# A perceiver layer with eight experts: residual rows sorted in the experts' order, weighted and scattered by each expert pass, and three weight parts used whole

## The reference

```python
x = x + xattn(layernorm(x), ctx, ctx, ...)       # 4 x 128 rows of 512, context 4 x 2048 x 256
x = x + dss(layernorm(x), ...)                   # long convolution
# expert layer, 512 tokens, 8 experts, 512 -> 2048 -> 512, everything in float32
xn = layernorm(x)
probs = softmax(xn @ w_gate + b_gate); route_p = max(probs); route_idx = argmax(probs)
h = relu(xn @ W1[e] + b1[e]); y = h @ W2[e] + b2[e]
out = x + y[route_idx] * route_p
```

## Time and profile before

| | us |
|---|---|
| median of 3 runs | 450.99 |
| lowest, highest | 450.6, 452.78 |
| the profiled execution, its own time | 450.92 |
| its span, first to last instruction | 449.1 |
| passes, first product to last | 188.4 to 431.6 |
| after the last product | 17.5 |

### The profile page before, as it was taken

How to read it: one execution, slowest core, us unless ns; L and a number is a source line. 1 busy time by engine, 2 the same in 40 slices (tenths; PEclk the granted TensorE clock), 3 DMA queues, 4 the chain that set the end, 5 groups by cost and what they waited for, 6 DMA issues and landing times.

```text
span 449.1 us, 5478 instructions
## 1 busy us (share of the span) xinstructions
PE 398.2 (89%) x1620; PEld 272.0 (61%) x1620; DVE 319.3 (71%) x506; ACT 249.9 (56%) x379; POOL 36.2 (8%) x41
## 2 busy tenths in 40 slices
PE   0999999999998975699998999999999999999940
PEld 0855567587863454576765667667576766757620
DVE  2778758795425867577877978799697879969702
ACT  4789778581000020575775757667685776757500
POOL 2100000000000010000201002010020201002022
PEclk9999999999999985989999999999999999999985
DMA  7995280874459400100169997698997979500006
GB/s 249 418 420 221 88 348 1 329 277 161 170 191 398 159 7 0 50 0 0 38 237 367 371 397 259 241 362 326 355 368 283 351 299 352 194 0 23 1 23 187
DMA packets 33695, 95.71 MB, mean 213 GB/s; under 512 B 2691, under 2 KB 3331, under 8 KB 32133
## 3 DMA queue, kind: packets, MB, share of 16 engines
q1 hardware_dynamic: 30900, 91.61, 54.8%
q0 software_dynamic: 1136, 3.67, 2.4%
q10 hardware_dynamic: 1632, 0.11, 0.3%
HBM read 91.72 MB, written 3.67 MB: 212 GB/s over the span
## 4 chain that ended last, share of the span: by engine, by line
PE 82%; DVE 6%; ACT 4%; DMA 3%; issue 3%; POOL 1%; DVEq 1%; SPq 0%; POOLq 0%; ACTq 0%
PE bank L1443 46%; PE bank L1281 6%; PE bank L1262 5%; PE bank L1458 4%; PE bank L1291 3%; PE bank L1215 2%; DMA ring<-in_wq_t 2%; PE bank L1327 2%; PE bank L1303 2%; PE bank L1270 2%; DVE work L1106 1%; DVE w_lo L1125 1%; ACT ring L518 1%; PE bank L1334 1%; PE bank L1424 1%
## 5 line engine op out<-in xcount | busy, mean ns | idle before, releaser
L1125 DVE TENSOR_TENSOR w_lo<-ring,w_hi 128x1024 fp32r<-128x1024 f32 x108 | 135.0, 1294 | 9.2 <-ACT w_hi L683 9.2
L683 ACT ACTIVATE w_hi<-ring 128x1024 fp32r<-128x1024 f32 x108 | 112.8, 1055 | 35.8 <-PE bank L1443 35.3
L1443 PE MATMUL bank<-ring,work 128*128 128x512 f32 x144 | 67.8, 603 | 0.0
L1443 PE MATMUL bank<-w_hi,x_hi 128*128 128x512 f32 x144 | 49.3, 424 | 5.1 <-DVE w_lo L1125 5.1
L1443 PE MATMUL bank<-w_hi,x_lo 128*128 128x512 f32 x144 | 45.2, 396 | 0.0
L1443 PE MATMUL bank<-w_lo,x_hi 128*128 128x512 f32 x144 | 45.1, 395 | 0.0
L1443 PEld LDWEIGHTS bank<-ring,work 128*128 128x128 f32 x144 | 25.8, 189 | 25.6 <-issue 23.3
L708 ACT ACTIVATE h_hi<-work 128x512 fp32r<-128x512 f32 x36 | 22.7, 631 | 26.5 <-DVE work L1112 25.9
L1193 POOL TENSOR_TENSOR small<-small,work 128x512 f32<-128x512 f32 x9 | 17.2, 1914 | 241.2 <-ACT small L689 241.2
L1443 PEld LDWEIGHTS bank<-w_hi,x_hi 128*128 128x128 f32 x144 | 26.7, 192 | 14.5 <-DVE w_lo L1125 8.0
L1106 DVE COPY work<-bank 128x512 f32<-128x512 f32 x18 | 12.4, 688 | 27.1 <-PE bank L1443 27.1
(11 more groups left out here) (184 smaller groups left out, 555.5 us busy)
## 6 DMA issues: line engine op xcount, KB each, us to landing
ring<-in_w SPq DMA_DIRECT2D x32, 2048.0 KB, 9.6
ring<-in_ctx_turned SPq DMA_DIRECT2D x4, 2048.0 KB, 12.2
ring<-in_ctx SPq DMA_DIRECT2D x4, 2048.0 KB, 14.2
y_rows<-small POOLq DMA_DIRECT2D x9, 256.0 KB, 5.3
work<-in_b SPq DMA_DIRECT2D x8, 256.0 KB, 5.6
ring<-in_wq_t SPq DMA_DIRECT2D x1, 1024.0 KB, 8.9
x_sb<-in_x SPq DMA_DIRECT2D x1, 1024.0 KB, 11.3
out<-x_sb SPq DMA_DIRECT2D x4, 256.0 KB, 3.0
```

What stands on the lines that cost most here:

```text
L683: act.activation(w_hi[:, n % NSPLIT, :, :], weight_part(e, n), ACT.Identity).then_inc(hi_ready, 1)
L1125: dve.tensor_tensor(w_lo[:, n % NSPLIT, :, :], weight_part(e, n), w_hi[:, n % NSPLIT, :, :], ALU.subtract).then_inc(lo_ready, 1)
L1443: ins = pe.matmul(dst, kept, moved, start=start and g == 0 and q == 0, stop=stop and g == 1 and q == len(terms) - 1)
```

## The change

1. **Rows.** `x_sb` becomes `x_ext`, 514 columns a row: the residual, the gate's probability and the token's number. After the router POOL scatters its four blocks to the DRAM tensor `sorted_rows` in the experts' order and waits for them. `y_rows`, the gathers, the four weighted additions and SP's four writes are gone.
2. **A pass.** After the pass before has been scattered, POOL loads this window's 128 rows of `sorted_rows` into `x_rows_w` (which is block 0 of `x_ext`). DVE adds probability times the expert's bias to them as the last step of a pass (`bias_added`). In the next pass ACT's copy of the result multiplies by the probability, POOL adds the row block, and scatters the sum by an indirect DMA to the result at the tokens' numbers. The padding rows have a number beyond the result and are skipped.
3. **Parts.** `WHOLE` is (6, 14, 15). Parts 12 and 13 are halved now, 14 is whole; `h_hi` and `h_lo` of block 3 are no longer made, and o3 waits for the relu.
4. **Waits.** The wait on the earlier output block stands in `block_may_copy` only where that block has a whole part; so the copy of h3 no longer waits for o1. The waits on `h_lo` of odd blocks count one a pass.

```diff
-WHOLE = (6, 12, 13, 15)
+WHOLE = (6, 14, 15)
...
-    y_rows = nc.dram_tensor("y_rows", ((NB + 1) * P, D), F32, kind="Internal").ap()
+    sorted_rows = nc.dram_tensor("sorted_rows", ((NB + 1) * P, D + 2), F32, kind="Internal").ap()
...
-        x_sb = sb("x_sb", [P, NB, D])
+        x_ext = sb("x_ext", [P, NB, D + 2])
+        x_sb = x_ext[:, :, 0:D]
+        x_rows_w = x_ext[:, 0, :]
...
         def block_may_copy(eng, p, w, k):
             wait_block(eng, w, "h", 2 * k + p)
-            eng.wait_ge(h_lo_ready[p], 2 * w + k + 1)
-            wait_block(eng, w, "o", 2 * k + p - 2)
+            if p == 0 or k == 1:
+                eng.wait_ge(h_lo_ready[p], 2 * w + k + 1 if p == 0 else w + 2)
+            before = 2 * k + p - 2
+            if not {2 * BLOCKS.index(("o", before % 4)) + g for g in range(2)}.isdisjoint(WHOLE):
+                wait_block(eng, w, "o", before)
...
# ScalarE: outputs_copy(w), and the end of its pass
                 act.wait_ge(rows_sent, 16 * w + 16)
-                act.activation(y_out, bank[:, Y_BANK, :], ACT.Identity).then_inc(y_copied, 1)
+                act.wait_ge(sorted_sent, 16 * NB)
+                act.wait_ge(x_rows_ready, w + 1)
+                act.activation(y_out, bank[:, Y_BANK, :], ACT.Identity, scale=x_rows_w[:, D:D + 1]).then_inc(y_copied, 1)
...
                         block_copy(w, 1)
+                        for n in range(12, 14):
+                            split_high(e, w, n)
                         block_relu(e, w, 1)
                         block_high(w, 2)
-                        for n in (14,):
-                            split_high(e, w, n)
-                        block_high(w, 3)
...
# VectorE
+            def bias_added(e, w):
+                dve.wait_ge(x_rows_loaded, 16 * w + 16)
+                dve.wait_ge(b2_loaded[e % NB2], 16 * (e // NB2 + 1))
+                dve.scalar_tensor_tensor(out=x_rows_w[:, 0:D], in0=b2_sb[e % NB2], scalar=x_rows_w[:, D:D + 1],
+                                         in1=x_rows_w[:, 0:D], op0=ALU.mult, op1=ALU.add).then_inc(x_rows_ready, 1)
...
                         block_copy(w, 1)
+                        for n in range(12, 14):
+                            low_part(e, w, n)
                         block_low(w, 2)
                         block_relu(e, w, 1)
-                        low_part(e, w, 14)
-                        block_low(w, 3)
+                        bias_added(e, w)
...
# GpSimd, after its 17 value_loads
+            pool.wait_ge(rows_ready, 2)
+            pool.wait_ge(prob_ready, 1)
+            for b in range(NB):
+                pool.indirect_dma_start(sorted_rows, bass.IndirectOffsetOnAxis(ap=row_i[:, b:b + 1], axis=0),
+                                        x_ext[:, b, :], None).then_inc(sorted_sent, 16)
+            pool.wait_ge(sorted_sent, 16 * NB)
...
                         first_row = window_row(offsets[e], w - bounds[e])
+                        pool.wait_ge(y_copied, w + 1)
+                        pool.wait_ge(rows_sent, 16 * w + 32)
+                        pool.dma_start(x_rows_w, sorted_rows[bass.ds(first_row, P), :]).then_inc(x_rows_loaded, 16)
+                        pool.wait_ge(x_rows_ready, w + 2)
                         pool.wait_ge(y_copied, w + 2)
-                        pool.tensor_tensor(y_out, y_out, b2_sb[e % NB2], ALU.add).then_inc(y_added, 1)
+                        pool.tensor_tensor(y_out, y_out, x_rows_w[:, 0:D], ALU.add).then_inc(y_added, 1)
                         pool.wait_ge(y_added, w + 2)
-                        pool.dma_start(y_rows[bass.ds(first_row, P), :], y_out).then_inc(rows_sent, 16)
+                        pool.tensor_tensor(rstd, m_half, m_half, ALU.mult)
+                        pool.indirect_dma_start(out, bass.IndirectOffsetOnAxis(ap=x_rows_w[:, D + 1:D + 2].bitcast(U32), axis=0),
+                                                y_out, None, bounds_check=NB * LQ - 1, oob_is_err=False) \
+                            .then_inc(rows_sent, 16)
             pool.wait_ge(rows_sent, 16 * bounds[NE] + 32)
...
# TensorE: output(e, w, i)
-                pe.wait_ge(h_lo_ready[p], 2 * w + k + 2)
+                if i == 3:
+                    pe.wait_ge(h_relu[p], 2 * w + k + 2)
+                else:
+                    pe.wait_ge(h_lo_ready[p], 2 * w + k + 2 if p == 0 else w + 2)
```

More of the change, by code:

```diff
@@ L58 @@
 for _name, _n in (("ident", P), ("ones", P), ("cos_f", P), ("sin_f", P), ("cos_t", P), ("sin_t", P),
-                  ("pick", P + BL - 1), ("own", HG), ("earlier", P), ("iota", P), ("blocks", NB), ("rank_e", NE),
+                  ("pick", P + BL - 1), ("own", HG), ("token", NB), ("earlier", P), ("iota", P), ("blocks", NB), ("rank_e", NE),
                   ("before_e", (NE + 1) * NE)):
@@ L63 @@
 TABLE_COLS = _at
-COLS = 172
+COLS = 148
 K1 = 16
@@ L200, in perceiver_layer @@
         by_group = small[:].rearrange("p (g n) -> p g n", n=2 * HG)
-        zeros = work[:, 0:D]
+        pad_rows = work[:, 0:D + 2]
         k_time = small[:, 0:D]
@@ L233, in perceiver_layer @@
         step_l, phase_c = times_c[:, 0:AH + BL], times_c[:, AH + BL:]
-        step_mag, step_ph = col(AH + BL), col(AH + BL)
+        step_mag, step_ph = col(AH + BL), step_l
         bn6, mv = col(6), col(2 * NB)
@@ L257, in perceiver_layer @@
         fmax = route(100, 4)
-        psum_e, prob = route(104, 4), route(108, 4)
+        psum_e = route(104, 4)
+        prob = x_ext[:, :, D:D + 1].rearrange("p b o -> p (b o)")
+        token = x_ext[:, :, D + 1:D + 2].rearrange("p b o -> p (b o)").bitcast(U32)
         rt1 = TABLES["sin_f"][0]
@@ L320, in perceiver_layer @@
         y_copied, y_added, rows_sent = sem("y_copied"), sem("y_added"), sem("rows_sent")
-        gathered = [sem(f"gathered{b}") for b in range(NB)]
-        result_ready, result_sent = sem("result_ready"), sem("result_sent")
+        sorted_sent, prob_ready = sem("sorted_sent"), sem("prob_ready")
+        x_rows_loaded, x_rows_ready = sem("x_rows_loaded"), sem("x_rows_ready")
         def weight_place(j):
@@ L481, in _ @@
                 next_b2(e)
[L482 to L485, removed]
         @block.scalar
@@ L706, in block_high @@
                 act.wait_ge(h_relu[p], 2 * w + k + 2)
-                wait_block(act, w, "o", i - 2)
+                wait_block(act, w, "o", i - 2 if p == 0 else i - 4)
                 act.activation(h_hi[:, p, :, :], hid[p].rearrange("p (m s) -> p m s", m=HB_CH), ACT.Identity) \
@@ L1080, in _ @@
             dve.tensor_copy(row_i, slot).then_inc(rows_ready, 1)
-            one_ahead = [*h_copied, *t_filled, *h_relu, *h_lo_ready, y_added]
+            dve.tensor_copy(token, table("token")).then_inc(rows_ready, 1)
+            one_ahead = [*h_copied, *t_filled, *h_relu, *h_lo_ready, y_added, x_rows_ready]
             for i, s in enumerate(one_ahead + PARTS * [parts_used]):
@@ L1118, in block_low @@
                 p, k = i % 2, i // 2
-                dve.wait_ge(h_hi_ready[p], 2 * w + k + 1)
+                dve.wait_ge(h_hi_ready[p], 2 * w + k + 1 if p == 0 else w + 1)
                 dve.tensor_tensor(h_lo[:, p, :, :], hid[p].rearrange("p (m s) -> p m s", m=HB_CH), h_hi[:, p, :, :],
@@ L1169, in inverse_root @@
                     .then_inc(rstd_ready, 1)
-            pool.memset(zeros, 0.0).then_inc(zeros_ready, 1)
-            pool.wait_ge(zeros_ready, 1)
+            pool.memset(pad_rows[:, 0:D + 1], 0.0).then_inc(zeros_ready, 1)
+            pool.memset(pad_rows[:, D + 1:D + 2], 1.0).then_inc(zeros_ready, 1)
+            pool.wait_ge(zeros_ready, 2)
             for i in range(2):
                 rows = slice(i * P // 2, (i + 1) * P // 2)
-                pool.dma_start(y_rows[NB * P:, :][rows], zeros[rows]).then_inc(rows_sent, 16)
+                pool.dma_start(sorted_rows[NB * P:, :][rows], pad_rows[rows]).then_inc(rows_sent, 16)
             pool.memset(a_tab[0:NS, :, steps_of(0, 1)], 1.0).then_inc(coarse_start, 1)
@@ L1514, in shape_tables @@
     put("blocks", P * np.arange(NB))
+    put("token", P * np.arange(NB)[None, :] + p[:, None])
     put("rank_e", NE - np.arange(NE))
```

13 lines of the change are left out of this document (2 added, 11 removed).

## The result

The changed kernel takes 440.17 us (median of four, 439.0 to 441.28); the kernel before took 451.51 beside it. The ratio is 0.9747 with a 95% interval of 0.9704 to 0.9789: faster, by 11.3 us. The forecast of 434.0 was 6.2 us too low; its range, 429.5 to 440.5, just held the median, while two of the four executions (441.13 and 441.28) lie above it. The profiled execution took 441.28, its span is 439.6.

The account below looks back on a forecast made before the run. TensorE, busy 89% of the span, was taken to bound the kernel. Span 449.1 - 8.5 (passes) - 0.9 (empty expert) - 10.6 (tail) + 3.0 (head) = 432.1, so 434.0 us measured; range 429.5 to 440.5.

Parts of the forecast that it names:

- D: DVE's order in a pass: the stall only moves, something else is as late as o1's wait; 440 us, chance 0.06.
- B: Head: four scatter issues stretched beside DVE's halvings, 3.8 us, plus part of the clock's 1.6; t0 past 201; 438 to 440, chance 0.14.
- The pass: Each pass, h0 to h0: 0.63 us saved before o2 and 0.31 behind it, 0.94 together, nine times 8.5.
- the parts' term: From o2's start into the next pass: two halved and two whole parts, 6.78 us instead of 7.09, 0.31 saved.
- Rival C: From t1 to o2: POOL's issue of the row load stretches DVE's chain, up to 0.95 each pass; 442 us, chance 0.05.
- Pass 2: Pass at the empty expert: of DVE's 1.48 us extra for passing it, the added lead hides 0.9.
- The tail: After the last product: write, gathers, additions and SP's writes go; 10.6 us saved (9.4 to 12.1) of 17.5.
- The head: Router to first pass: ACT's first copy waits for scatters behind 17 register loads; t0 at 198.7, 3.0 us lost once.
- The four issues: POOL's scatters at the head: first to last issue 3.8 us, as four indirect issues took before.
- The bounds 0 to 4.5: Loss at the head: 0 if the landing at 191.6 hides completely, 4.5 us if the last lands after 4.9.
- Rival E: DVE waits for its rows: scatter and load take over 16.0 us, slower than before; at 19, 458 us; chance 0.03.
- 1.0 + 0.4 of bound: Rows' margin in a pass: loaded by +20.3 us at latest, DVE needs them at +20.7 and may lose 1.0 more.

Follow-up runs that it names:

- the two runs without the standstill: Changed kernel with ScalarE's copy not waiting for the four scatters, 433.57 us; changed kernel with the scatters issued before GpSimd's 17 register loads, 432.7 us.

## Why the prediction was right in its range and 6 us off

In the profiled spans the sum is 7.5 us short: 4.9 at the head, 2.1 in front of pass 0 and 0.75 at the tail, less 0.25 in passes 1 to 8. That the range held the median is partly luck: its upper end, set to hold D and most of B, is 0.3 us above it, the head left its own bounds, and the 2.1 us in front of pass 0 were in no case of mine.

**The pass: right.** From t1 to o2 I had 10.62 and it is 10.59 (425.37 - 414.78), with each DVE step where the sum put it. From o2 to the next h0 it takes 5.93 where the parts' term gives 5.92. The pass is 25.73 against 25.64, since h0 to t1 takes 9.22 and not 9.10: the fp32r products became slower by their operands' place, and no step of mine had that. Rival D falls: the release before o2 is DVE's h_lo. Rival C falls: no DVE step between t1 and o2 is longer than in rows 3.

**Pass 2: right in kind, too small.** The added lead hid more than 0.9: DVE's `x_hi` behind the empty expert starts behind 1.66 of idle time instead of 2.38, and between other passes behind 0.16 to 0.20 instead of 0.90; I had kept both as they were, and why they shrank wasn't tested. Passes 1 and 2 took 28.07 and 26.93 us before and 25.75 and 25.77 after, 3.5 less where I had 2.8. Passes 1 to 8 gave 8.65 in all, 8.4 predicted.

**Attribution: a step missed.** I priced the wait at 0.63 and the parts at 0.31 a pass. The wait alone is worth 1.2 in a late pass and the parts nothing there, since their halvings stand in front of h_lo. The sum held, since I had laid both edits into one schedule; only the split of the result was wrong.

**The tail: right, 0.75 short.** After ACT (0.69, 0.09 longer with a scale from SBUF) POOL starts at 432.81. The scatter is issued 2.95 behind the last product (434.90 - 431.95), 3.1 predicted. The span ends 4.7 behind the issue; I took 3.7, a gather's median, and 0.1. The bound, 4.9, held.

**The head: the step that failed.** Its parts, in the profile's own times, with the later start of 2.07:

- POOL's register loads: the 17 stand in the chain from 179.77 to 189.73, 10.0 us or 0.59 each; 0.6 predicted. Right. The first scatter follows 0.82 behind them, for which I had nothing.
- The four issues: 190.55 to 196.29 is 5.7; I took 3.8 from gathers, three of whose four were issued while DVE was idle. Two of the scatters, beside halvings, took 1.97 and 1.89. That is rival B's mechanism, at two issues of four: +1.9. An issue of this kind takes 1.0 alone and 1.9 beside halvings, while a plain write's is 0.56 in both cases (in rows 8 beside them, and the same at 434.32 with DVE idle). The Trainium skill (SBUF — State Buffer, "Who interferes with whom") has DVE instructions with two SBUF inputs contend with GpSimd instructions that read SBUF. The trace is in line with it for the indirect issue; that this rule is the cause was not tested.
- The landing: 199.90 - 196.29 = 3.6 up to ACT's start, 3.46 of it the DMA; 3.7 predicted. Right.
- So ACT's copy came 10 us late, TensorE stood for 5.12, and t0 came 5.3 late instead of 3.0.
- During the standstill, at 202, the granted clock fell to 0.50, and it came back only at 208.8: pairs of products started 0.85 apart instead of 0.47. With it the rest of the pass took 22.33 us, and 19.73 in the run with the scatters first, which has no standstill. That is 2.6 us; I had named at most 1.6 and taken 0.

3.0 predicted, 7.9 paid (34.85 against 26.98 for pass 0). With the later start taken off, t0 stands at 200.95, where I had set the sign for rival B (past 201), and the total is at the upper end of B's 438 to 440. So the outcome is nearer to B, to which I gave 0.14, than to the forecast with its 0.58. The bounds 0 to 4.5 held the landing alone: the stretched issues and the clock stood outside them, and I took both at nothing. How long the lower clock lasts varies: in the profiled execution with 32 bytes more, which has the same head, it ended at 205.5, and pass 0 took 32.81. So the price lies between 5.8 and 7.9 us, and the two runs without the standstill got 6.6 and 7.5 back in their medians.

**The start: not in the sum.** In the profiled run the first weights landed 1.9 us later and everything behind with them. That isn't this execution alone: pass 0 begins at 189.1 to 190.9 in all twelve kernels with `x_ext`, and at 188.4 and 188.3 in the two with `x_sb`. In the eleven other kernels with `x_ext` this landing took 9.4 to 10.9, in the two with `x_sb` 8.9 and 9.0. So part of it may belong to the rows. I had left this stretch at nothing without a reason, and its cause stays open.

**Rival E: real, not reached.** The changed kernel waited once for its rows, 0.7 in pass 2. Others with the same POOL work waited there for 0.3 to 2.1, or not at all. With two multiplications more on POOL it lost 8 us, with four it was slower than before. The margin was thinner than my 1.0 + 0.4 of bound suggests: the nine scatters of the result landed 7.8 at the median and 8.5 at most after issue, above the 7.3 I took as the longest.

## What to carry to other kernels

Before a wait is added in front of an early instruction, count everything that stands ahead of what it waits for on the other queue, register loads too: here a copy whose result nobody needed yet held up the whole first pass. Cost two edits of one stretch each alone as well as together; nearly all of this gain was one wait, and the other edit took back in the queue what it saved on TensorE, until one of its halvings was moved. Price a standstill of TensorE above its length: here 5.3 us of delay brought 2.6 more at the lower clock.

## What the runs showed of the hardware

- In a standstill of 5.1 us TensorE's granted clock fell to the lower of its two levels (1.2 instead of 2.4 GHz) and stayed there for the first 5.8 us of work behind it (products 0.43 us apart instead of 0.23), worth 2.6 us. Behind a standstill of 2.5 us, in the run with four multiplications, it was low for 3.4 us.
- A register load from SBUF took GpSimd 0.59 us each, 17 in a row.
- An indirect DMA's issue took 1.0 us alone and 1.5 to 2.0 beside halvings on VectorE, while a plain DMA's issue took 0.56 to 0.6 in both cases. A short instruction before it can take part of that waiting in its place (one spacer and the issue: 1.06 + 1.82; five and the issue: 2.63 + 1.03).
- fp32r products on `x_hi` and `x_lo` ran about 2% slower when the tensors behind the residual lay 32 or 64 bytes further on, and at full pace again with them 8192 bytes lower than in the kernel before. Weight loads took 188 ns at the median in all cases.
